# Attention and FFN kernel on one core: values, first scores and the high parts of block 3 in another order at the front of a tile

## The reference

```python
x = L0_attn_x                                            # (1, 4096, 512)
qkv = x @ w_qkv.T                                        # heads of 32, rotary q and k
scores = einsum('bhqd,bhkd->bhqk', q, k) * scale         # only 0 <= row - column < 64
out = softmax(scores) @ v @ w_out.T
x = layernorm(x + out)
gate, up = silu((x @ w_gate) * s_gate), (x @ w_up) * s_up
x = layernorm(x + ((gate * up) @ w_down) * s_down)
```

## Time and profile before

| | |
|---|---|
| median of 3 runs | 1165.49 us (1164.7 to 1165.99) |
| the profiled execution | 1166.12 us, its span 1164.3 us |
| busy in the span | PE 99%, DVE 84%, ACT 53%, POOL 52% |
| granted TensorE clock | 0.998 of full speed over the span |
| share of the chain that ended last | PE 78%, DVE 7%, issue 6% |

### The profile page before, as it was taken

How to read it: one execution, slowest core, us unless ns; L and a number is a source line. 1 busy time by engine, 2 the same in 40 slices (tenths; PEclk the granted TensorE clock), 3 DMA queues, 4 the chain that set the end, 5 groups by cost and what they waited for, 6 DMA issues and landing times.

```text
span 1164.3 us, 25889 instructions
## 1 busy us (share of the span) xinstructions
PE 1148.5 (99%) x8577; PEld 595.0 (51%) x8577; DVE 976.0 (84%) x2797; ACT 622.3 (53%) x1724; POOL 600.5 (52%) x570
## 2 busy tenths in 40 slices
PE   9999999999999999999999999999999999999998
PEld 4344446464464644646455464554645545464444
DVE  7889998889997899878999789887898978986434
ACT  3863883159920689117980279702796038950330
POOL 0775684356731667326771367614676245752330
PEclk9999999999999999999999999999999999999999
DMA  9999786357672585717757077561874627644000
GB/s 295 161 186 242 140 172 147 85 100 139 121 174 56 96 139 112 175 40 124 138 98 166 37 142 127 97 160 38 151 123 91 166 58 136 126 74 109 19 1 37
DMA packets 353042, 139.59 MB, mean 120 GB/s; under 512 B 309968, under 2 KB 332624, under 8 KB 352912
## 3 DMA queue, kind: packets, MB, share of 16 engines
q1 hardware_dynamic: 334976, 106.86, 49.6%
q0 software_dynamic: 10800, 18.09, 5.3%
q10 hardware_dynamic: 7136, 12.93, 3.2%
HBM read 36.13 MB, written 9.18 MB: 39 GB/s over the span
## 4 chain that ended last, share of the span: by engine, by line
PE 78%; DVE 7%; issue 6%; POOL 3%; DMA 3%; ACT 2%; SPq 1%; ACTq 0%; DVEq 0%; POOLq 0%
PE bank L906 52%; PE bank L1217 17%; PE bank L916 3%; PE bank L1143 2%; DMA xT_sb<-xT_sb 2%; DVE v_own L1794 2%; POOL xT_sb L690 1%; ACT bank L1457 1%; PE bank L1123 1%; ACT fuse L1356 1%; POOL fuse L695 1%; DVE ffn_tmp L1844 1%; DMA qkT<-fuse 1%; DVE bank L1831 1%; DVE probs L1809 1%
## 5 line engine op out<-in xcount | busy, mean ns | idle before, releaser
L906 PE MATMUL bank<-x1T,wg 128*128 128x512 f16 (+1 forms) x1032 | 242.5, 378 | 1.1 <-DVE ffn_tmp L1844 1.1
L906 PE MATMUL bank<-x1T,wu 128*128 128x512 f16 x1024 | 241.9, 379 | 0.0
L1457 ACT ACTIVATE bank<-bank,neg_max,qk_scale 128x128 f32<-128x128 f32 x512 | 220.4, 434 | 23.5 <-DVE neg_max L1837 22.4
L1217 PE MATMUL bank<-wd,fuse 128*128 128x512 f16 (+2 forms) x1056 | 223.3, 373 | 0.7 <-DVE y L1892 0.6
L695 POOL TENSOR_TENSOR fuse<-ffn_tmp,fuse 128x512 f16<-128x512 f32 x128 | 149.7, 1170 | 96.5 <-ACT fuse L1356 96.2
L800 POOL TENSOR_TENSOR fuse<-fuse 128x512 f16<-128x512 f32 x116 | 142.6, 1266 | 88.3 <-ACT fuse L1356 86.1
L1217 PEld LDWEIGHTS bank<-wd,fuse 128*128 128x128 f16 x1056 | 101.6, 98 | 118.7 <-DVE y L1892 1.6
L906 PEld LDWEIGHTS bank<-x1T,wu 128*128 128x128 f16 x1024 | 100.2, 98 | 120.6
L690 POOL TENSOR_TENSOR xT_sb<-probs,xT_sb 128x512 f16<-128x512 f32 x112 | 131.0, 1170 | 52.2 <-ACT xT_sb L1356 52.0
L906 PEld LDWEIGHTS bank<-x1T,wg 128*128 128x128 f16 x1032 | 96.4, 98 | 112.7 <-DVE ffn_tmp L1844 2.0
L1366 ACT ACTIVATE ffn_tmp<-bank,tanh_scale 128x512 f32<-128x512 f32 x128 | 88.7, 693 | 65.9 <-PE bank L906 42.2
(11 more groups left out here) (258 smaller groups left out, 1846.7 us busy)
## 6 DMA issues: line engine op xcount, KB each, us to landing
v_cross<-v_own SPq DMA_DIRECT2D x64, 128.0 KB, 2.4
out<-x ACTq DMA_DIRECT2D x31, 256.0 KB, 2.0
xT_sb<-xT SPq DMA_DIRECT2D x30, 256.0 KB, 4.9
qkT<-x SPq DMA_DIRECT2D x28, 256.0 KB, 3.2
wg<-w_gate POOLq DMA_DIRECT2D x7, 1024.0 KB, 5.7
v_cross<-kept_v_weights ACTq DMA_DIRECT2D x5, 768.0 KB, 7.5
wu<-w_up POOLq DMA_DIRECT2D x7, 512.0 KB, 6.3
wqkv<-w_qkvT SPq DMA_DIRECT2D x8, 256.0 KB, 6.2
```

The costliest lines, as they stand in the source:

```text
L906: last = pe.matmul(dst, lhsT, rhs, start=(i == 0 and not onto), stop=(i == len(pairs) - 1), skip_group_check=onto)
L1217: last = pe.matmul(dst[:, cols], fuse[:, s, z, rows], wd[:, s, cols], start=(s == 0 and z == 0), stop=(s == STEPS - 1 and z == 1))
L1457: last = act.activation(unit, unit, ACT.Exp, bias=neg_max[:, s % 2, h // 3, h % 3:h % 3 + 1], scale=qk_scale[:, 2:3], accum_out=row_sum[:, ...
```

## The change

In tiles 2 to 7, on three engines (nothing is added to the arithmetic, and the DMAs stay as they are):

- PE: `values_second` of pair 0 moves ahead of `values_fifth` of pair 1. The first two score steps move ahead of the last six quarter products; before, only two quarter products came behind them. `V_SECOND` and `V_SEVENTH` become pairs of numbers, since the place in the order is no longer the same for both pairs.
- ACT: all of block 2's high parts move ahead of the copies of the fifth (pair 1) and of the seventh (pair 0). Block 3's high parts come in two halves. The first half stands ahead of the copy of the sixth of pair 1, the second behind the first exponentials and the high parts of values 0 and 1. The copy of the seventh of pair 1 now stands behind the first exponentials.
- DVE: one `add_v` ahead of the first two maxima instead of two; the others between the weights and the low parts. A new wait on PE's seventh product of pair 1 stands ahead of the first weights, whose output lies where that product's operand was.

```diff
-        V_FIRST, V_FIFTH, V_SIXTH, V_THIRD, V_SEVENTH, V_SECOND, V_FOURTH = range(7)
+        V_FIRST, V_FIFTH, V_SIXTH, V_THIRD, V_FOURTH = 0, 1, 2, 3, 6
+        V_SECOND, V_SEVENTH = (4, 5), (5, 4)
@@ PE
             def project_values(a):
                 values_sixth(a, 0)
                 values_third(a, 0)
+                values_second(a, 0)
                 values_fifth(a, 1)
                 values_seventh(a, 0)
+                scores(a, 0, True)
+                scores(a, 1, True)
                 values_sixth(a, 1)
-                values_second(a, 0)
                 values_fourth(a, 0)
                 values_third(a, 1)
                 values_seventh(a, 1)
-                scores(a, 0, True)
-                scores(a, 1, True)
                 values_second(a, 1)
                 values_fourth(a, 1)
@@ ACT
                 elif attn:
                     keep_values_sixth(a, 0)
+                    split_high(a, 2, ffn)
                     keep_values_fifth(a, 1)
                     keep_values_seventh(a, 0)
+                    split_high(a, 3, ffn, range(2))
                     keep_values_sixth(a, 1)
-                    split_high(a, 2, ffn)
+                    exponentials(a, 0, ffn)
                     keep_values_seventh(a, 1)
-                    split_high(a, 3, ffn)
-                    exponentials(a, 0, ffn)
                     keep_v(a, 0, ffn)
                     keep_v(a, 1, ffn)
+                    split_high(a, 3, ffn, range(2, 4))
                     exponentials(a, 1, ffn)
@@ DVE
                     add_v(a, 0)
-                    add_v(a, 1)
                     for s in range(2):
                         maxima(a, s, ffn)
                         bias(a, s)
-                        add_v(a, 2 + s)
+                    add_v(a, 1)
+                    wait(v_product[1], dve, a - 2, V_SEVENTH[1])
                     weights(a, 0, ffn)
-                    for j in range(2):
-                        split_v(a, j, ffn)
+                    add_v(a, 2)
+                    split_v(a, 0, ffn)
+                    add_v(a, NB - 1)
+                    split_v(a, 1, ffn)
                     weights(a, 1, ffn)
```

More of the change, by code:

```diff
@@ L1408, in keep_values_seventh @@
             def keep_values_seventh(a, i):
-                keep_value_product(a, i, v_rows(2 * i + 1)[:, 0:HALF_EMB], v_places(i)[3], V_SEVENTH)
+                keep_value_product(a, i, v_rows(2 * i + 1)[:, 0:HALF_EMB], v_places(i)[3], V_SEVENTH[i])
             def carry_v(a):
@@ L1786, in add_v @@
                 wait(v_products_kept[i], dve, a - 2, 2 + back)
-                wait(v_product[i], dve, a - 2, V_FOURTH if back else V_SECOND)
+                wait(v_product[i], dve, a - 2, V_FOURTH if back else V_SECOND[i])
                 done(v_added, dve.scalar_tensor_tensor(out=v_rows(j), in0=bank32[j], scalar=v_scale[:, 1:2],
```

## The result

The changed kernel takes 1170.47 us (median of 5 runs, 1169.57 to 1171.24) against 1165.49 (5 runs, 1164.67 to 1166.15): a ratio of 1.0044, 95% interval 1.0029 to 1.0059. So it is slower, by 5.0 us. The profiled execution has a span of 1168.4 us (before 1164.3), and the granted clock is 0.999.

A forecast was written before the change was run, and what follows sets the result against it. PE, busy 99% of the span, was taken as the bound. New waits of 8.3 us less 6.0 of old ones gave +2.3 on the 1165.49 median: 1167.8 us, range 1163.0 to 1170.8 (forecast alone 1166.0 to 1169.5).

The forecast's parts named there:

- old waits: PE's waits A, B and C in tiles 2 to 7 before the change, together 6.0 us, expected to go.
- A: PE's gate product of step 2 starts late behind the scores: 0.24 us six times, 1.5 us; expected to go.
- C: PE's weighted sum starts late behind its predecessor: 0.58 us in tile 3, 3.1 over six tiles; expected to go.
- B: Second half of PE's score pair waits for step 2's weights: about 0.3 us, 1.4 in all; expected to go.
- first new wait: Pair 1's seventh product on PE waits for ACT's sixth copy, held by block 1's landing; 6.1 us, tiles 2-6.
- The second: PE's fourth product waits for ACT's copy of the seventh, behind the first exponentials; 0.3 to 0.4 us a tile, 2.3 in all.
- restart of 0.10: Extra time of PE's first product after each new wait: 0.1 us taken, bounds nothing to 0.2, eleven times.
- cost foreseen for the contention: DVE's low parts of values beside POOL: 1.64 instead of 0.68 us; one hidden, a second costs 0.96 of lead a tile.
- Rival 2: Slower: DVE and ACT move with PE's late products, C stays, A and B go; +5.4, 1170.9 us; chance 0.16.
- Rival 1: Faster: the landing is no obstacle on ACT, both new waits vanish; 3 to 6 us won, 1159.5 to 1162.5; chance 0.15.
- Rival 3: No difference: the wait at the seventh product comes, that at the fourth does not; +0.1, 1165.6 us; chance 0.14.
- Rival 4: PE's pauses drop its clock to 1.2 GHz, costing 3.5 us in five tiles; 1185 us; chance 0.01.

## Why the prediction was right, and where it was off

**The mechanism was right.** Both new waits are at the places and for the reasons named. The runs with the copy of the sixth ahead, and with block 3 behind the exponentials, show that the landing is what ScalarE waits for, since the pause moves with it or goes. The old waits went as predicted: A and C are nil, and B is too. By the spacing, at most 0.2 us of the 6.0 are left. ScalarE's first tanh is 17.05 us behind the tile's mark (17.51 before), DVE's gate 18.21 (19.02): leads of 0.46 and 0.81, where 0.3 to 0.6 was foreseen.

**The step that was off is the size of the first new wait**: "The first wait is 2.5 less that difference: 1.1, 1.4, 1.3, 1.1, 1.2, and none in tile 7. Sum 6.1." Measured, with the restart: 1.98, 1.27, 2.23, 1.79, 1.68 and none, 8.95 us. The second was right (2.3 forecast, 2.45 measured), and so was the restart of 0.10. New waits come to 11.4 instead of 8.4, and 11.4 less the 5.75 that went is 5.6. The span rose by only 4.1: some 1.1 us of pauses at the spreading of the next maximum in tile 5 were fewer this time, and tile 2 began 0.5 us sooner. Neither was forecast, and no run changed either. So that the measured time is still inside the range owes something to luck.

I took the landing from the kernel before and wrote "Nothing in the change makes it earlier". I did not ask what makes it *later*. From its issue to its landing the transfer took 4.9, 6.1, 5.9, 6.0, 6.1 and 4.9 us in tiles 2 to 7 before, and 5.8, 6.0, 6.8, 6.8, 6.7 and 4.7 after, with issues within 0.15 us of the same places behind the tile's mark. Counted from the mark, the landings of tiles 2 to 6 are 2.9 us later together, the whole of what was missing. It agrees tile by tile: in tile 3 the landing is not later, and the pause was 1.27 against 1.4 foreseen. In tile 6 of the changed kernel (the mark is 821.76):

```profile
DMA  9999999999800000000000000000000000000000
GB/s 282 290 286 303 282 290 286 303 282 286 202 0 0 0 0 0 0 0 0 0 0 0 0 0 0 0 0 0 0 0 0 0 0 0 0 0 0 0 0 0
DMA packets 725, 0.19 MB, mean 77 GB/s; under 512 B 724, under 2 KB 724, under 8 KB 724
...
q14 instruction: 1, 0.01, 0.8%
```

```profile
830.85 1.15 ACT L1357 ACTIVATE fuse<-fuse 128x512 f16<-128x512 f32 x2 [2.58 <-DMA qkT<-fuse]
```

The window is 828.8 to 831.2, in 40 slices. The data is through at 829.45, yet ACT is released only at 830.85. In the trace 15 of the transfer's 16 completion marks have come by 830.01, and the last comes at 830.77. An 8 KB transfer of the instruction queue starts at 829.42, as the last packets of the transfer end, and its packet takes 0.31 us. In the kernel before, the same instruction transfer comes 9.1 to 9.4 us behind the mark, behind the landing, and the 16 marks lie within 0.2 us.

The run with VectorE's order undone separates this from the rest. The other engines have the same programs, but the instruction transfer moves from 7.7 to 8.2 us behind the mark to 9.8, in every tile from 2 to 6. The landings fall back to what they were before (4.9, 6.2, 5.3, 6.1, 6.2 and 4.8 us from the issue), and the first pause from 8.4 to 4.7 us in all. In the run with TensorE's order alone, which has VectorE's old order too, the instruction transfer is at 9.8 in tiles 2 to 5 and 10.1 in tile 6, as was expected before it ran. In the kernels that keep the maxima ahead of `add_v(1)` it is at 7.3 to 8.3. So it goes with VectorE's order, though no trace says whose instructions it carries.

The spread of 7.3 to 8.3 follows the turning transfer: in all eleven of these kernels, tiles 2 to 6, the instruction packet starts 0.01 to 0.08 us before the transfer's last packet ends, as if it stood behind it. In 42 of these 55 tiles the last mark is then 0.76 to 0.81 us behind the one before it, in the other 13 (tile 3 of the changed kernel among them) 0.08 to 0.19. In the three kernels with VectorE's old order the packet starts at least 1.0 us after the transfer's last packet, and in none of the 15 tiles is the last mark late. The late marks of tiles 2, 4, 5 and 6 of the changed kernel come to 3.1 us, about the 2.9 by which its landings moved.

The section "Instruction fetch mechanics" of the page "Runtime: NRT & Kernel Launch" of the Trainium skill says that each engine's sequencer fetches its instructions over a DMA queue of its own while it executes. The trace agrees in so far as it has instruction queues beside those of the data (q8 with 78 packets and q14 with 52 in the changed kernel); it has two of them and does not name their engines. That the late completion mark is caused by sharing a queue's engine with the instruction transfer is the reading of these times; no run changed the instruction transfer alone, and the trace does not tell which packets share an engine.

**A second omission did not show in the number.** I called VectorE's new order "the same four instructions". It is free here, as predicted, but only because the exponentials are early. `add_v(3)` had become a condition of the gate product of step 1, and cost 13.1 us when ScalarE's order was undone. What stands behind a wait was asked of the new wait on the seventh product, not of the sums that were moved.

**The contention.** The section "Who interferes with whom" of the page "SBUF — State Buffer" of the Trainium skill says that a VectorE instruction with two SBUF inputs contends with a GpSimd instruction that reads SBUF. The traces agree in part: 1.65 and 1.64 against 0.68 us for the same residuals. But in the kernel before the residual of values 0 (406.14) lay inside POOL's stretch of the earlier trace rows and took 0.77. The sums, whose one input is in PSUM, took 0.74 in both. In the changed kernel one residual lay at the start of POOL's stretch (406.41, POOL from 406.74 to 409.68) and took 0.68, the next (407.67), inside it, 0.98. So the cost foreseen for the contention, "a second costs 0.96 of lead", did not come there. It came in the experiments. What decides between 0.7 and 1.65 stays open.

**The rivals.** Rival 2 gives the measured time within 0.5 us (1170.9), but not by its way. The others did not move with PE, C did not stay, and the tanh kept its lead. Rival 1 (the landing no obstacle) is excluded by the 2.17 us of ACT's idle time; the run without the landing in the way also shows that its gain was not to be had by that alone. Rival 3 falls with the second pauses.

Rival 4, the clock, did not come in the changed kernel: the granted clock was 0.999 with pauses of up to 2.1 us. But it is not excluded as the forecast had it, from one stretch of the earlier trace rows. In the profiled executions of four experiments the clock fell to 0.50 behind a pause: once in the run with the copy of the sixth ahead (tile 4, pause 2.13) and in that with VectorE's order undone (tile 7, 2.05), twice with ScalarE's order undone (tiles 2 and 3, 2.24), and in every tile from 2 to 7 with the scores put back. A single fall cost 1.5 to 1.7 us. Tile 4 of the changed kernel has a pause of 2.13 too and no fall, and tiles 4 to 7 with ScalarE's order undone have the same 2.24 as tiles 2 and 3. So a pause of this length may cost it or not. It also fell at 65.3 and 64.5 us of the first two kernels with block 3's high parts between the copies and the exponentials, right behind the stretch of the earlier trace rows and with nothing changed there: that row, at 1.00, was one outcome of two.

**One of the signs was wrong.** "the first tanh of a tile should stand 7.7 us behind PE's first scores there plus or minus 0.5". It is 11.1 (398.71 to 409.83), and it was 8.1 before (400.78 to 408.90). The scores move ahead and the tanh does not, as my own replay had it: 7.7 was taken from the old place of the scores. The replay's tanh was right and the sign written from it was not.

## What to carry to other kernels

An engine that runs in order may work ahead only on what is certain to be ready. A wait for a transfer put in front of a copy on which TensorE depends gives the whole lateness to TensorE, and moving one copy past it hands the wait to the next one. When a stall goes, look for the instruction that two engines later has a second reader, here the sum that frees a bank, and put it into the idle time ahead of the wait instead of behind it. A landing time read from the old trace is not a constant. Here it moved with VectorE's order by up to 0.9 us although the transfer was issued at the same place, so a sum that rests on a few tenths of it needs them in its range. And a sum of pauses is not the whole price once they come near 2 us: look at the granted clock behind them.

## What the runs showed of the hardware

- An 8 KB instruction transfer that started at the tail of a turning transfer (0.01 to 0.08 us before its last packet ended) went with a last completion mark 0.8 us behind the other 15 in 42 of 55 tiles. Where it started 1.0 us or more after that packet, the mark was late in none of 15. A 16 KB one stands 4.2 to 5.3 us behind the tile's mark in tiles 2 to 6 of both kernels. In the kernel before, block 1's second transfer lands at 8.4 to 8.7 there, and at 7.2 in tile 7, which has no instruction transfer at that place; that the one causes the other is not shown.
- A reordering of VectorE's program moved the 8 KB instruction transfer by 1.6 to 2.1 us against the other engines, without any instruction added to them.
- GpSimd beside VectorE's residual (both operands in SBUF) made it 1.65 instead of 0.68 us in several kernels, but 0.77 and 0.98 in two other places. POOL slowed less: four low parts took 4.50 us with no residual beside them, 5.2 to 5.4 in other stretches.
- One pause of PE of 2.05 to 2.24 us in a tile was followed by a fall of the granted clock to 0.50 in four tiles, and in others of the same length it was not; a fall cost 1.5 to 1.7 us. With two pauses a tile of up to 2.5 us by the view of waits, 21 us in all (scores put back), it fell in each tile from 2 to 7, and its mean over the span was 0.987.
